# A graph network kernel on one core: first rows in two loads, one queue ahead of the other, and W5's sum ahead of the biases

## What is computed

```python
h = x
for _ in range(3):
    a = einsum('nm,bmd->bnd', adj, h)
    av = concatenate([a, a], axis=-1)
    z = sigmoid(av @ w3.T + b3 + h @ u3.T + bu3)
    r = sigmoid(av @ w4.T + b4 + h @ u3.T + bu3)
    hv = tanh(av @ w5.T + b5 + (r * h) @ u5.T + bu5)
    h = (1.0 - z) * h + z * hv
out = layernorm(x + h)
```

## Time and profile before

| | us |
|---|---|
| median of 3 runs | 735.25 |
| lowest and highest | 735.22, 735.64 |
| the profiled execution, its own time | 734.97 |
| its span, first to last instruction | 732.9 |

### The profile page before, as it was taken

The page is one execution under the profiler, slowest core; times in us unless marked ns, Lnnn a source line. Parts: engine busy times, 40 slices in busy tenths (PEclk is TensorE's granted clock), DMA queues, the critical chain, the costliest instruction groups (busy, mean ns, idle before and its releaser), DMA issues.

```text
span 732.9 us, 9687 instructions
## 1 busy us (share of the span) xinstructions
PE 726.1 (99%) x3237; PEld 602.3 (82%) x3237; DVE 635.7 (87%) x932; ACT 419.4 (57%) x647; POOL 29.9 (4%) x71
## 2 busy tenths in 40 slices
PE   9999999999999999999999999999999999999997
PEld 7888888888888888888888888888888888888886
DVE  6788898889998888898999888899899987899887
ACT  5645655465666654565566754565556664565546
POOL 0000000000010000000011000000011000000013
PEclk9999999999999999999999999999999999999999
DMA  8145454446766445445567445544467544544442
GB/s 345 61 145 168 136 184 143 140 148 186 237 225 194 160 148 172 152 137 167 188 237 229 156 139 172 184 140 134 163 203 254 195 159 143 164 132 134 142 145 116
DMA packets 74183, 124.13 MB, mean 169 GB/s; under 512 B 8368, under 2 KB 55472, under 8 KB 74160
## 3 DMA queue, kind: packets, MB, share of 16 engines
q1 hardware_dynamic: 72144, 116.43, 48.8%
q10 hardware_dynamic: 2016, 7.41, 2.8%
HBM read 67.18 MB, written 56.62 MB: 169 GB/s over the span
## 4 chain that ended last, share of the span: by engine, by line
PE 98%; DVE 1%; ACT 0%; issue 0%; POOLq 0%; POOL 0%; DVEq 0%
PE ps_g L420 17%; PE ps_g L418 17%; PE ps_g L419 17%; PE ps_v L420 12%; PE ps_v L418 12%; PE ps_v L419 12%; PE ps_a L420 3%; PE ps_a L418 3%; PE ps_a L419 3%; PE ps_g L510 1%; PE ps_a L438 1%; PE ps_g L549 0%; PE ps_v L510 0%; DVE dz L1072 0%; DVE stats L1037 0%
## 5 line engine op out<-in xcount | busy, mean ns | idle before, releaser
L685 ACT ACTIVATE ps_v<-ps_v,bias 128x512 f32<-128x512 f32 x94 | 62.2, 662 | 182.7 <-PE ps_v L420 182.7
L418 PE MATMUL ps_g<-aT_hi,wt_lo 128*128 128x512 f32 (+1 forms) x380 | 147.1, 387 | 0.0
L420 PE MATMUL ps_g<-aT_hi,wt_hi 128*128 128x512 f32 (+1 forms) x380 | 147.0, 387 | 0.0
L419 PE MATMUL ps_g<-aT_lo,wt_hi 128*128 128x512 f32 (+1 forms) x380 | 147.0, 387 | 0.0
L724 ACT ACTIVATE z<-ps_g,bias 128x512 f32<-128x512 f32 x94 | 64.8, 690 | 95.0 <-PE ps_g L420 94.6
L418 PEld LDWEIGHTS ps_g<-aT_hi,wt_lo 128*128 128x128 f32 x380 | 71.3, 188 | 14.6
L419 PEld LDWEIGHTS ps_g<-aT_lo,wt_hi 128*128 128x128 f32 x380 | 71.3, 188 | 14.5
L420 PEld LDWEIGHTS ps_g<-aT_hi,wt_hi 128*128 128x128 f32 x380 | 71.3, 188 | 14.5
L870 DVE TENSOR_TENSOR aT_lo<-aT,aT_hi 128x1024 fp32r<-128x1024 f32 x46 | 56.4, 1225 | 30.4 <-ACT aT_hi L660 30.4
L860 DVE STREAM_TRANSPOSE ab<-ps_a 128x1024 f32<-128x1024 f32 x46 | 57.4, 1249 | 23.5 <-PE ps_a L420 22.3
L418 PE MATMUL ps_v<-rh_hi,wt_lo 128*128 128x512 f32 x192 | 74.7, 389 | 0.0
(11 more groups left out here) (126 smaller groups left out, 1237.0 us busy)
## 6 DMA issues: line engine op xcount, KB each, us to landing
turned_a<-ab SPq DMA_DIRECT2D x46, 512.0 KB, 3.7
aT<-turned_a SPq DMA_DIRECT2D x184, 128.0 KB, 3.0
turned_h<-hb SPq DMA_DIRECT2D x46, 512.0 KB, 2.6
hn<-turned_h SPq DMA_DIRECT2D x184, 128.0 KB, 3.0
x_in<-in_x_rows SPq DMA_DIRECT2D x14, 512.0 KB, 4.6
xT<-in_x_cols SPq DMA_DIRECT2D x12, 512.0 KB, 4.3
out<-y ACTq DMA_DIRECT2D x12, 512.0 KB, 3.6
wide<-in_w_t SPq DMA_DIRECT2D x3, 512.0 KB, 6.6
```

The lines of the kernel that those rows point to most:

```text
L418: nc.tensor.matmul(dst, lhs_lo, rhs_hi, start=first, stop=False, skip_group_check=True)
L419: nc.tensor.matmul(dst, lhs_hi, rhs_lo, start=False, stop=False, skip_group_check=True)
L420: return nc.tensor.matmul(dst, lhs_hi, rhs_hi, start=False, stop=last, skip_group_check=True)
L685: nc.scalar.activation(ps_v[:, oc, :], ps_v[:, oc, :], ACT.Tanh, bias=bias[:, BV, oc:oc + 1]).then_inc(v_ready, 1)
```

## The change

ScalarE's first load holds only the first two graphs' rows and the adjacency. A second load brings the other two graphs' rows into the free half of `y[0]`. Then comes the load of U3 with half of the state, and a semaphore `lead_issued` is raised. SyncE waits for it in place of `neg_half_ready`, and so issues all its loads behind the three. The first half of the first aggregation waits for the first load, the second half for the second. The warm-up has 11 transposes in place of 13. On VectorE the sum of W5 stands before the wait for the biases and their three adds.

```diff
--- before.py
+++ after.py
@@ -56,7 +56,7 @@
 EPS = 1e-5
 
 
-def build(nc, x_rows, first_rows, second_rows, lead, x_cols, w3_t, w4_t, w5_t, u5_t, biases, out_rows):
+def build(nc, x_rows, first_rows, first_rest, second_rows, lead, x_cols, w3_t, w4_t, w5_t, u5_t, biases, out_rows):
     N, B, D = out_rows.shape
     ROWS = 512
     GB = ROWS // N
@@ -99,8 +99,8 @@
         bias = sb("bias", [P, 3, C])
         wt_hi = [sb(f"wt_hi{k}", [P, C, D], F32R) for k in range(5)]
         wt_lo = [sb(f"wt_lo{k}", [P, C, D], F32R) for k in range(5)]
-        first_in = sb("first_in", [P, GB * D + N])
-        adjT = first_in[:, GB * D:GB * D + N]
+        first_in = sb("first_in", [P, HB * D + N])
+        adjT = first_in[:, HB * D:HB * D + N]
         W3, W4, W5, U3, U5 = range(5)
         BZ, BR, BV = range(3)
 
@@ -123,7 +123,11 @@
         aT = sb("aT", [P, QUADS, LINE])
         z = [sb(f"z{k}", [P, C, ROWS]) for k in range(2)]
         y = [sb(f"y{k}", [P, GB, D]) for k in range(2)]
-        x_first = [first_in[:, 0:GB * D].rearrange("p (b d) -> p b d", b=GB), y[1]]
+
+        def x_first(j, b, cols):
+            if j == 0 and b < HB:
+                return first_in[:, b * D + cols.start:b * D + cols.stop]
+            return y[j][:, b, cols]
         y_tail = sb("y_tail", [P, GB, D])
 
 
@@ -181,7 +185,8 @@
 
 
         x_loaded = [sem(f"x_loaded{k}") for k in range(2)]
-        rows_first = sem("rows_first")
+        rows_first, rows_rest = sem("rows_first"), sem("rows_rest")
+        lead_issued = sem("lead_issued")
         stored = [sem(f"stored{k}") for k in range(2)]
 
 
@@ -372,13 +377,13 @@
             def load_wide(k):
                 sp.dma_start(wide[k][:, :, :, :], wide_in[k]).then_inc(w_loaded[k], DMA)
 
-            sp.wait_ge(neg_half_ready, 1)
+            sp.wait_ge(lead_issued, 1)
             sp.dma_start(xT[0][:, 1, :], x_cols[0, :, 1, :]).then_inc(xT_first[1], DMA)
             load_wide(W4)
             sp.dma_start(bias_in[:, :, :], biases).then_inc(bias_loaded, DMA)
             load_wide(W5)
             load_wide(W3)
-            sp.dma_start(x_first[1][:, :, :], second_rows).then_inc(rows_second, DMA)
+            sp.dma_start(y[1][:, :, :], second_rows).then_inc(rows_second, DMA)
             load_cols(0, 1)
             sp.dma_start(square[1][:, :, :], u5_t).then_inc(w_loaded[U5], DMA)
             load_rows(0, 2)
@@ -429,14 +434,17 @@
 
             def first_aggregate(j):
 
-                pe.wait_ge(rows_second if j == 1 else rows_first, DMA)
                 for hf in range(2):
+                    if j == 0:
+                        pe.wait_ge((rows_first, rows_rest)[hf], DMA)
+                    elif hf == 0:
+                        pe.wait_ge(rows_second, DMA)
                     bank = by_chunk(ps_a[:, hf, :])
                     for bb in range(HB):
                         b = hf * HB + bb
                         for c in range(C):
                             done = nc.tensor.matmul(bank[:, c, bb * N:(bb + 1) * N],
-                                                    x_first[j][:, b, c * P:(c + 1) * P],
+                                                    x_first(j, b, slice(c * P, (c + 1) * P)),
                                                     adjT[:, :], start=True, stop=True)
                     done.then_inc(a_ready, 1)
 
@@ -551,7 +559,7 @@
             def first_round():
 
                 pe.wait_ge(ident_ready, 1)
-                keep_warm(13)
+                keep_warm(11)
                 first_aggregate(0)
                 first_u()
                 first_dense(ps_g[0], W4, False, True, rpre_ready)
@@ -745,7 +753,9 @@
                 nc.scalar.copy(wt_hi[k][:, :, :], weight(k)[:, :, :]).then_inc(wt_hi_ready, 1)
 
             act.dma_start(first_in[:, :], first_rows).then_inc(rows_first, DMA)
+            act.dma_start(y[0][:, HB:GB, :], first_rest).then_inc(rows_rest, DMA)
             act.dma_start(lead_in[:, 0:C * D + ROWS], lead).then_inc(lead_loaded, DMA)
+            act.sem_inc(lead_issued, 1)
 
             act.wait_ge(neg_half_ready, 1)
             nc.scalar.activation(table_probe[:, :], neg_half[:, :], ACT.Sigmoid)
@@ -999,11 +1009,11 @@
             for hf in range(2):
                 first_a_low(0, hf)
             weight_low(W4)
+            sum_halves(W5)
             dve.wait_ge(bias_loaded, DMA)
             for b, (l, r) in ((BZ, (0, 1)), (BR, (2, 1)), (BV, (3, 4))):
                 nc.vector.tensor_tensor(bias[:, b, :], bias_in[:, l, :], bias_in[:, r, :],
                                         ALU.add).then_inc(bias_ready, 1)
-            sum_halves(W5)
             sum_halves(W3)
             weight_low(W5)
             subtract_r()
@@ -1179,7 +1189,8 @@
     bias_names = ("w3", "u3", "w4", "w5", "u5")
     laid = {
         "x_rows": x.reshape(B // GB, GB, N, C, QUADS, BLK).transpose(0, 2, 4, 3, 1, 5).reshape(B // GB, N, GB * D),
-        "first_rows": np.concatenate([x[0:GB].transpose(1, 0, 2).reshape(N, GB * D), adj.T], axis=1),
+        "first_rows": np.concatenate([x[0:GB // 2].transpose(1, 0, 2).reshape(N, GB * D // 2), adj.T], axis=1),
+        "first_rest": x[GB // 2:GB].transpose(1, 0, 2),
         "second_rows": x[GB:2 * GB].transpose(1, 0, 2),
         "lead": np.concatenate([features_first(w("u3"), 1).reshape(P, C * D),
                                 x[0:GB].reshape(GB * N, C, P)[:, 0, :].T], axis=1),
```

## The result

The changed kernel takes 738.29 us (median of 6 runs, 737.82 to 740.51) against 735.25 us before: the ratio is 1.0043, 95% interval 1.0033 to 1.0054. The forecast was 735.16 us. The kernel is 3.0 us slower, where I had expected no change, and slower than the 735.8 us at which my range ended.

A forecast was written before the change was run, and what follows sets the result against it. TensorE, on 98% of the chain, was taken to bound the kernel, with only its first 12 us able to count. Start 0 and W5 -0.09 gave -0.09 us: 734.88, plus 0.28 to the median, 735.16 us; range 734.7 to 735.8.

The forecast's parts named there:

- is covered by some 2 us, and W4 stays at 7.7: Start loads: SyncE issues 0.5 us later, but its data waited 3 us behind ACT's anyway, so W4's landing does not move.
- W4 lands later: Rival, start loads: one more load ahead of W4 delays it by 0 to 0.45 us; for 0.4, 735.55 us; chance 0.13.
- the sum: Whole kernel: 0 (start) - 0.09 (W5) = -0.09 us, giving 735.16 us.
- U3 to land at 5.8 as before: Start loads: U3 with half of the state, 1.16 issue + 4.6 to landing = 5.8 us.
- nothing behind the first 12 us can count: TensorE after 12.4 us: no weight load waits, so only time won or lost in the first 12 us reaches the end.
- Eleven transposes, aggregation from 3.94 us: TensorE's start: two transposes fewer, aggregation from 3.9 us, 0.6 us sooner; slow first half, fast second, through at 6.5, 0.4 sooner.
- The second `hT_lo` behind W4's sum: Twelve-product chain's last pair: TensorE's earlier gain is spent waiting there; start priced at 0, ends 0 and 0.4 us.
- W5's move: W5's sum ahead of the biases on DVE: 0.2 us wait gone, products 2.72 us instead of 2.81, gain 0.09 us.
- The clock: Rival, TensorE's start: pace rises after 5.6 us, each microsecond later costing 0.49 us; 736.4 at 3.5 us delay; chance 0.07.
- My bound of 0.9 us: TensorE's clock rise: three times of before lie 0.42 us apart, so its moment can vary by no more than 0.9 us.
- the order of the two queues: DMA engines at the start: SyncE's queue moved nothing in its first 3 us, against the skill's rule of taking turns.

The follow-up runs named there:

- e11: Kernel before, with ten idle semaphore steps ahead of SyncE's first load, issued at 2.15 us instead of 1.55; 736.66 us.
- e10: Changed kernel with two more transposes put between the first aggregation and U3's products (11 and 2); 736.89 us.
- e3: Changed kernel with the 13 warm-up transposes of before instead of 11, loads untouched; 736.89 us.
- e5: Kernel before with 11 warm-up transposes instead of 13 and nothing else; 736.84 us, ratio 1.0022.
- e9: Kernel before with 11 transposes instead of 13, run once more for its trace; 736.73 us.
- e1: Changed kernel, but SyncE waits for GpSimd's constant as before instead of for ScalarE's three loads; 738.49 us.
- e12: Kernel before, with SyncE held only until ScalarE's first issue, so its first load goes at 1.21 us instead of 1.55; 735.87 us.
- e13: Kernel before, with seven idle steps in SyncE instead of the wait for GpSimd's constant, first load at 1.28 us; 735.81 us.
- e6: Kernel before with only the first rows in two loads (13 transposes, SyncE not held back, biases first); 736.63 us, ratio 1.0024.
- e4: Kernel before with only W5's sum moved ahead of the biases; 735.53 us, ratio 1.0000.
- e7: Kernel before, with SyncE issuing ScalarE's two loads as well, ahead of its own, all in one queue; 736.07 us.
- e8: Changed kernel with 13 transposes and all loads issued by SyncE in one queue, in the changed order; 736.52 us.

## Why the prediction was wrong

*The step that failed first* is the sentence that SyncE's later issue "is covered by some 2 us, and W4 stays at 7.7". From the earlier trace rows I read that data issued at 1.55 us moves only from 4.6 on, and took the three microseconds between as slack. They are not. e11 moves the issue of SyncE's loads (twelve at the start, not the fourteen that I had counted) to 2.15 us and nothing else, W4 lands at 9.0, and it costs 1.5 us (736.66 against 735.19 in its session). The changed kernel issues at 2.17, and its trace places 1.5 us at the start. That a load's data has to wait for the engines does not show that the load would be ready to run if it were issued later. The rival "W4 lands later" had the right place, but I priced it at 0.4 us at most, from the time that an issue takes, and gave it 0.13. Both this rival and the sum took U3 to land at 5.8 as before; it did so in e10, but in the changed kernel and in e3 one share came at 6.7 and 7.7.

*The second is a term that the sum did not have.* Taking out two transposes costs 1.5 us by itself (e5: 736.84 against 735.35), and e9's trace has it in a pause of 1.5 us, 710 us later. I had counted their removal as a gain or as nothing. The two together make 3.0 us on 735.25; 738.29 was measured. With the transposes back (e3) the changed kernel is 1.6 us above before, which is the first part alone. What is left is below what these runs can tell. My sentence that nothing behind the first 12 us can count rested on the waits for semaphores, and this pause is none.

*What held.* Eleven transposes, aggregation from 3.94 us, the first eight multiplies slow and the second eight fast (1.06 us for them in the timeline), through at 6.6. The second `hT_lo` behind W4's sum is the bound of the start, and what TensorE gains ahead of it is spent waiting. W5's move takes its wait away and brings 2.81 to 2.72 us; nothing behind it became late. The clock did not decide, as I had thought likely: the pace changed near 5.6 us in both traces. My bound of 0.9 us on how far this moment can vary, taken from three times of before, was wrong, though: in e1 it came over 2 us later (last section). The slower side that I had drawn up (the clock) was the wrong mechanism, and the pause was in no rival.

*On the order of the two queues* I had read from the trace of before that the engines do not take turns between them. That holds for its loads, issued 0.4 us apart, but not in general: in e12 and e13, with issues 0.04 and 0.12 us apart, both queues move side by side. In e6, at 0.09 us, the load issued first lands first. What decides between the two was not found. The split made U3 the third of ScalarE's loads; without the hold SyncE's load passes it (+1.3 us, e6), with the hold SyncE's loads are late (e3: +1.6 us). Splitting the first rows lost either way.

*No version beat the kernel before.* e4 equals it.

## What to carry to other kernels

A load that waits for the DMA engines is not thereby free to be issued later: before moving an issue, look at the stretch behind it for idle engines, and shift the issue alone by a few idle steps to get its price. Adding or removing instructions of an engine whose program runs past a loop can move the moment at which its next instructions are brought in; when a small edit costs more than its trace stretch explains, look far from it for a pause put down to "issue", and put the same number of instructions back elsewhere to test it. Where executions of one kernel differ (before took 735.0 to 736.5 us), take a second trace before you explain the first.

## What the runs showed of the hardware

*Loads issued later in a full queue landed later by more than the shift:* 0.6 us later in issue, 1.3 us in landing of W4 (e11), with engines idle for a quarter of the time from 5.0 to 6.5 us; in the changed kernel, issued at 2.17, for over a third. The lateness is uneven over the 16 engines: W4's shares land from 7.6 to 9.0 us in e11 and from 7.4 to 8.9 in e7, against 7.35 to 7.75 before. One queue for all loads (e8) filled the idle time, but at 258 GB/s. Why the engines get to these loads late was not found.

*Instructions of one program came in at two different times:* some 5 or 8 us behind the end of the loop, in the same kernel (e5 and e9). By its times, one execution in eleven had the sooner one. What picks one was not settled; with 13 transposes, or 11 and 2, no trace had the later one.

*The moment at which TensorE's pace rises differs from execution to execution.* The second eight multiplies of the first aggregation, the same instructions at 5.4 to 5.9 us, took this long in the changed kernel with 13 transposes and in e1:

```profile
5.41 1.06 PE L446 MATMUL ps_a<-first_in,y 128*128 128x128 f32 x8
```

```profile
5.88 1.91 PE L445 MATMUL ps_a<-first_in,y 128*128 128x128 f32 x8
```

The first runs at the pace of the 2.4 GHz level throughout, the second at that of 1.2 GHz, with TensorE fed since 1.52 us in both, but for at most 0.3 us before the rows came. It cost nothing in e1, since U3's parts came later still. The Trainium skill ("TensorE: Matmul & The Clock Gate", Part 1) says that this moment differs between runs, and the traces agree.
